# A graph network's second pass: another order of the turn on three engines, and step values loaded once per loop turn

## The chip, the cores and the metric

The kernel runs on 1 core of one Trainium2 chip. The metric is the device time of one execution in microseconds, as the median of 3 runs. Engines are called PE (TensorE), DVE (VectorE), ACT (ScalarE), POOL (GpSimd) and SP (SyncE).

## The reference

Four graph layers follow one another over 6,250 nodes and 206,250 edges sorted by `dst`. Each ends in a residual and a layer norm over 128 channels.

```python
x = _layernorm(x + _L0_gnn_ref(x, edge_index, edge_attr_128, ...))     # attention per edge, sum by dst
x = _layernorm(x + _L1_gnn_ref(x, edge_index_t, ...))                  # second layer: sums by src
x = _layernorm(x + _L2_gnn_ref(x, edge_index, edge_attr_128, ...))     # sum of edge features by src, small MLP
x = _layernorm(x + _L3_gnn_ref(x, ...))                                # top 8 of the edges of each src
```

The second layer needs, for each edge, the transformed row of one end and a sum over the edges that share the other end:

```python
h = jnp.matmul(node_states, kernel)
scores = jnp.exp(jnp.clip(leaky_relu(score_dst[dst] + score_src[src]), -2.0, 2.0))
out = jax.ops.segment_sum(h[src] * attention_norm[:, None], dst, num_segments=n_nodes)
```

(In this layer `dst` is `edges[:, 0]`, the kernel's `src`.) So the kernel must bring the edges from one order into the other. The part that does it, `stage_move`, is the one called the second pass here.

## The kernel before

Edges lie in tiles of 128, and 4 tiles are a group: there are 403 groups (GE). Nodes lie in 49 blocks of 128. Sorted edges touch their blocks in order, so a pass over pairs of group and block has 403 + 48 = 451 steps (KE). A table in SBUF, `steps`, holds for each step its group (row 0), its block (row 1) and its slot (row 2); an engine that needs one of these numbers for an address reads it into a register.

All loops are written with `pipeline(eng, n, *parts, ring=R)`. A part is `(function, lag)` or `(function, lag, items)`. In turn t an engine calls, in the order in which the parts are listed, each function for item t - lag. The middle of a loop runs as a hardware loop whose body is R turns; `u` is the item's place in the ring. Each engine works its own list in order and waits on semaphores that the others raise.

`stage_move` has two strands in one turn. The first ranks edges by their other end: one-hot tiles on DVE (`onehots`), their transposes and counts on PE (`counts`), the copy of the transposes on ACT (`turned`), running counts split into three bf16 parts (`running` on DVE, `high` on ACT, `below_high` on DVE, `middle` on ACT, `below_middle` on DVE), products on PE (`same`, `lookups`), and the choice of the place (`earlier`, `choose`, `position` on DVE, `index` on ACT). The second expands a node's row to its edges: ACT issues a DMA that broadcasts 512 keys to 128 partitions (`spread`, into 4 buffers `m_keys`), DVE compares them (`hot`), PE multiplies (`expand`), DVE adds the product into a slot of `m_rows` (`fill`), ACT adds three numbers (`put`). SP loads edge features into one of 8 slots (`load`, which raises `s_free`) and tells POOL when a group is complete (`ready`). POOL scatters it to DRAM by 4 indirect DMAs of 128 rows. The waits that the argument uses:

```python
spread: act.wait_ge(s_hot, k - U + 1)      # U = 4: the key buffer is free
turned: act.wait_ge(s_cnt, g + 1)          # PE counts(g) is done
expand: pe.wait_ge(s_add, k - 1); pe.wait_ge(s_hot, k + 1)   # fill(k - 2), hot(k)
hot:    dve.wait_ge(s_key[u], use * 16 + 16)
fill:   dve.wait_ge(s_got, k + 1); dve.wait_ge(s_free, g + 1)
below_middle: dve.wait_ge(s_middle, g + 1)
```

Two other loops read step values: `stage_aggregate` (first layer, 451 steps: SP loads, POOL weighs, DVE makes one-hots in `prepare` and adds in `add`, ACT copies, PE sums), and the last loop of `stage_last_layer`. There DVE keeps the block number of `prepare` for `add` where both fall into one loop body (class `Blocks`), and reads it again where not.

## Time and profile before

| | us |
|---|---|
| median of 3 runs | 14784.25 (14783.6 to 14784.43) |
| the profiled execution's own time | 14750.02 |
| its span in the profile | 14748.2 |

The span is the time from the first to the last instruction of one profiled execution. The execution's own time is 1.8 us longer than its span, and 34.2 us shorter than the median of the runs.

### The profile page before, as it was taken

What the parts mean: (1) busy time and instruction counts of PE and PEld (TensorE: products, weight loads), DVE (VectorE), ACT (ScalarE), POOL (GpSimd) and SP (SyncE); (2) the same over time, 40 slices, a digit from 0 to 9 for tenths busy, and PEclk for the clock granted to TensorE, in tenths of its full rate; (3) what the DMA queues carried; (4) which work ended last, traced back from release to release, by engine and by line L of the source; (5) the groups of instructions that cost most, each with busy time, mean ns of one, the idle gap of its engine ahead of it and who ended that gap; (6) DMA issues with size and microseconds to landing.
All of it is one profiled execution on the core that took longest, in us unless ns stands there. A gap on an engine that the chain in (4) does not pass through costs nothing. (4 is left out here: it accounts for less than half of the span.)

```text
span 14748.2 us, 216662 instructions
## 1 busy us (share of the span) xinstructions
PE 7244.2 (49%) x43137; PEld 6163.1 (42%) x43138; DVE 7073.5 (48%) x13194; ACT 1344.8 (9%) x4579; POOL 6702.6 (45%) x7772
## 2 busy tenths in 40 slices
PE   6999995673222222222222222223599578207543
PEld 4787774562222222222222222223366367206433
DVE  6444445776222222222222222222488678997535
ACT  1111111111000000000000000000011100001000
POOL 3777771663222222222222222225588057897773
PEclk9999998996555555555555555555799689657655
DMA  4777773451111111111111111114998069318654
GB/s 131 204 207 205 205 204 87 137 153 58 60 59 62 59 62 61 60 62 59 61 59 61 59 62 59 60 59 153 163 257 257 10 179 259 102 38 225 189 157 124
DMA packets 2114489, 1742.91 MB, mean 118 GB/s; under 512 B 377267, under 2 KB 1838644, under 8 KB 2114212
## 3 DMA queue, kind: packets, MB, share of 16 engines
q1 hardware_dynamic: 1220182, 819.70, 19.1%
q10 hardware_dynamic: 708032, 472.39, 12.2%
q0 software_dynamic: 186160, 449.72, 11.1%
q14 instruction: 96, 0.79, 0.0%
q8 instruction: 19, 0.31, 0.0%
HBM read 1289.54 MB, written 453.29 MB: 118 GB/s over the span
## 5 line engine op out<-in xcount | busy, mean ns | idle before, releaser
L1125 POOL DMA_INDIRECT sorted<-m_rows,srci x1612 | 1569.9, 974 | 5166.8 <-SPq L1112 4731.6
L1181 PE MATMUL m_psx<-held,m_hot 128*128 x3608 | 939.7, 441 | 4740.7 <-DVE m_rows L1335 4740.7
L1181 PEld LDWEIGHTS m_psx<-held,m_hot 128*128 128x128 f32 x3608 | 807.9, 329 | 4816.2 <-issue 4816.1
L1324 DVE TENSOR_SCALAR m_hot<-m_keys,node 128x512 f32<-128x512 int32 x451 | 225.7, 500 | 4583.0 <-DMA m_keys<-dst_row 4569.8
L1577 POOL DMA_INDIRECT z_xg<-table,srci x1664 | 2082.5, 1252 | 507.2 <-issue 507.2
L443 POOL DMA_INDIRECT g_xg<-table,srci x1612 | 1607.0, 997 | 491.1 <-issue 461.6
L1637 PE MATMUL z_ps<-z_wrow,z_oh 128*128 128x132 f32 x3712 | 757.8, 372 | 619.1 <-DVE z_wrow L1790 313.9
L462 PE MATMUL g_psg<-g_wg,g_eT 128*128 128x136 f32 x3224 | 1027.5, 474 | 0.0
L1452 PE MATMUL n_ps<-n_row,n_oh 128*128 128x257 f32 x3712 | 899.0, 391 | 249.4 <-DVE n_row L1428 203.4
L1637 PEld LDWEIGHTS z_ps<-z_wrow,z_oh 128*128 128x128 f32 x3712 | 666.7, 269 | 710.2 <-issue 670.2
L479 PE MATMUL g_psx<-scores,g_hot 128*128 x3608 | 840.2, 362 | 92.4 <-DVE e_score L568 87.0
L1452 PEld LDWEIGHTS n_ps<-n_row,n_oh 128*128 128x128 f32 x3712 | 670.9, 190 | 477.4 <-issue 347.6
L479 PEld LDWEIGHTS g_psx<-scores,g_hot 128*128 128x128 f32 x3608 | 806.7, 329 | 117.9 <-issue 115.1
L462 PEld LDWEIGHTS g_psg<-g_wg,g_eT 128*128 128x128 f32 x3224 | 769.3, 324 | 191.0 <-issue 191.0
L798 POOL TENSOR_TENSOR ag_wrow<-ag_buf,e_score 128x512 f32<-128x512 f32 x451 | 543.2, 1209 | 581.2 <-DMA ag_buf<-gated 359.4
L1206 ACT ACTIVATE m_ohtb<-m_pst 128x512 bf16<-128x512 bf16 x403 | 240.6, 597 | 5634.9 <-PE m_psu L1144 5634.9
L873 PE MATMUL ag_ps<-ag_wrow,ag_oh 128*128 128x136 f32 x3608 | 547.4, 299 | 233.2 <-DVE ag_oh L833 223.3
L1609 PE MATMUL z_ps<-z_tab,z_ohlo 128*128 128x200 bf16 x4992 | 601.3, 250 | 77.1 <-DVE z_e L1729 71.1
L541 DVE TENSOR_TENSOR g_y<-g_gate,g_xg 128x512 f32<-128x512 f32 x403 | 280.2, 695 | 732.5 <-DMA g_xg<-table,srci 731.5
L873 PEld LDWEIGHTS ag_ps<-ag_wrow,ag_oh 128*128 128x128 f32 x3608 | 466.0, 197 | 314.6 <-issue 197.0
L1171 PE MATMUL m_psl<-m_part,m_ohtb 128*128 128x100 bf16 x4836 | 582.8, 285 | 0.0
L833 DVE SCALAR_TENSOR_TENSOR ag_oh<-iota,blk,keys 128x512 f32<-128x512 f32 x451 | 470.6, 1044 | 181.6 <-PE ag_ps L873 97.3
(404 smaller groups left out, 13807.4 us busy)
## 6 DMA issues: line engine op xcount, KB each, us to landing
n_row<-sorted SPq DMA_DIRECT2D x464, 520.0 KB
z_buf<-gathered ACTq DMA_DIRECT2D x464, 256.0 KB, 3.6
g_keys<-dst_row ACTq DMA_DIRECT2D x451, 256.0 KB
ag_buf<-gated SPq DMA_DIRECT2D x451, 256.0 KB, 2.8
m_keys<-dst_row ACTq DMA_DIRECT2D x451, 256.0 KB, 3.7
gathered<-z_xg SPq DMA_DIRECT2D x416, 256.0 KB
gated<-g_y SPq DMA_DIRECT2D x403, 256.0 KB
g_eT<-in_attr_t SPq DMA_DIRECT2D x402, 256.0 KB
```

The lines of the kernel that those rows point to most:

```text
L443: nc.gpsimd.indirect_dma_start(out=xg[:, u, j, :], out_offset=None, in_=v.table[:, :], in_offset=bass.IndirectOffsetOnAxis(ap=v.srci[:, t: ...
L462: last = nc.tensor.matmul(psg[u % 2][:, h, j * W:(j + 1) * W], eT[:, u, (h * H + j) * P:(h * H + j + 1) * P], wg[:, :], start=False, stop= ...
L479: last = nc.tensor.matmul(psx[u % 2][:, j * X8:(j + 1) * X8], hot_t[:, u, j * P:(j + 1) * P], flat(v.scores[:, ds(b, 1), :]), start=True, ...
L798: engine.tensor_tensor(wrow[:, u, :, 0:C].rearrange("p t (h c) -> p t h c", h=heads), buf[:, u, :, :].rearrange("p t (h c) -> p t h c", h= ...
L873: last = nc.tensor.matmul(ps[u % 4][:, 0:width], oh[:, u, j, :], wrow[:, u, j, 0:width], start=(j == 0), stop=(j == G - 1))
L1125: nc.gpsimd.indirect_dma_start(out=v.sorted[:, :], out_offset=bass.IndirectOffsetOnAxis(ap=place[:, t:t + 1], axis=0), in_=rows[:, u, j, : ...
L1171: nc.tensor.matmul(to, ohtb[:, u, j * P:(j + 1) * P], before, start=(n == 0), stop=False)
L1181: last = nc.tensor.matmul(psx[u % 2][:, j // 2, (j % 2) * WH:(j % 2 + 1) * WH], hot_t[:, u, j * P:(j + 1) * P], flat(held[:, ds(b, 1), :]) ...
L1452: last = nc.tensor.matmul(ps[u % 4][:, 0:ROW], oh[:, u, j, :], row[:, u, j, 0:ROW], start=(j == 0), stop=(j == G - 1))
L1577: nc.gpsimd.indirect_dma_start(out=xg[:, u, j, :], out_offset=None, in_=v.table[:, :], in_offset=bass.IndirectOffsetOnAxis(ap=v.dsti[:, t: ...
L1609: nc.tensor.matmul(to, ohlo[:, u, edges], tab[:, n, :, :], start=(n == 0), stop=False)
L1637: last = nc.tensor.matmul(bank[u % 4 // 2][:, u % 2, 0:width], oh[:, u, j, :], wrow[:, u, j, 0:width], start=(j == 0), stop=(j == G - 1))
```

## The change

**Orders in `stage_move`.** On ACT `turned` goes from lag 0 to 2, `high` from 1 to 2, `middle` from 2 to 3, `index` from 5 to 6, `put` from 6 to 7; `spread` stays at 0 and first. On PE `expand` moves from the head of the turn to its end. On DVE `fill` moves from the end of the turn to second place. **Step values.** Class `StepRow` replaces single reads on the engines named below: at `u == 0` one instruction reads the values for all R turns of the loop body and for the `back` items before them. Code outside the hardware loop still reads one value at a time. PE's `expand` and SP's `ready` in `stage_move`, `stage_gate` and `stage_neighbours` keep their single reads.

```diff
-class Blocks:
...
+class StepRow:
+    def __init__(self, nc, eng, steps, row, top, back, ring, waited=False):
+        self.nc, self.eng, self.steps, self.row, self.top = nc, eng, steps, row, top
+        self.back, self.ring = back, ring
+        self.sure = None if waited else "stage_steps keeps groups and blocks in their ranges"
+
+    def turn(self, k, u):
+        if isinstance(k, int) or u:
+            return
+        _, self.values = self.nc.values_load_multi_w_load_instructions(
+            self.steps[0:1, self.row, ds(k - self.back, self.ring + self.back)], engines=[self.eng.engine], min_val=0,
+            max_val=self.top, skip_runtime_bounds_check_because=self.sure)
+
+    def at(self, k, u, lag=0):
+        if isinstance(k, int):
+            return self.eng.value_load(self.steps[0:1, self.row, ds(k, 1)], min_val=0, max_val=self.top)
+        return self.values[(u + lag) % self.ring - lag + self.back]
...
@@ stage_aggregate (the same form on SP, POOL, DVE, ACT; and on ACT and DVE in stage_last_layer)
-                blocks = Blocks(nc, dve, steps, groups, 3, R)
+                group = StepRow(nc, dve, steps, 0, groups - 1, 0, R)
+                node = StepRow(nc, dve, steps, 1, NBX - 1, 3, R)
...
@@ stage_move
-                pipeline(pe, GE, (expand, 1, KE), (lookups, 3), (same, 1), (counts, 0), ring=R)
+                pipeline(pe, GE, (lookups, 3), (same, 1), (counts, 0), (expand, 1, KE), ring=R)
...
+                ahead = StepRow(nc, act, steps, 0, GE - 1, 7, R, waited=True)
+                slots = StepRow(nc, act, steps, 2, S - 1, 7, R)
+
                 def spread(k, u, use):
-                    g, _ = step_of(nc, act, steps, k, GE)
+                    ahead.turn(k, u)
+                    slots.turn(k, u)
+                    g = ahead.at(k, u)
...
                 def put(k, u, use):
-                    g = act.value_load(steps[0:1, 0, ds(k, 1)], min_val=0, max_val=GE - 1)
-                    slot = act.value_load(steps[0:1, 2, ds(k, 1)], min_val=0, max_val=S - 1)
+                    g, slot = ahead.at(k, u, 7), slots.at(k, u, 7)
...
-                pipeline(act, GE, (spread, 0, KE), (turned, 0), (high, 1), (middle, 2), (index, 5), (put, 6, KE), ring=R)
+                pipeline(act, GE, (spread, 0, KE), (turned, 2), (high, 2), (middle, 3), (index, 6), (put, 7, KE), ring=R)
...
+                node = StepRow(nc, dve, steps, 1, NBX - 1, 0, R)
+                group, slots = StepRow(nc, dve, steps, 0, GE - 1, 3, R, waited=True), StepRow(nc, dve, steps, 2, S - 1, 3, R)
...
-                pipeline(dve, GE, (hot, 0, KE), (below_middle, 3), (choose, 4), (onehots, 0), (running, 1),
-                         (below_high, 2), (earlier, 2), (position, 4), (fill, 3, KE), ring=R)
+                pipeline(dve, GE, (hot, 0, KE), (fill, 3, KE), (below_middle, 3), (choose, 4), (onehots, 0), (running, 1),
+                         (below_high, 2), (earlier, 2), (position, 4), ring=R)
```

In ACT's loop body of `stage_move`, before, these instructions stand between the slot number's read (L1224), `put` (L1229), the next turn's `spread` (L343 reads, L1198 issues) and its `turned` (L1206). TENSOR_LOAD reads `steps` into a register, ISA and REGISTER_ALU work on registers.

```order
L1224 TENSOR_LOAD steps_e
L1224 ISA x2
L1225 REGISTER_ALU
L1229 ISA x2
L1229 ACTIVATE m_rows<-m_facts 128x4x3
L343 ISA
L343 TENSOR_LOAD steps_e
L343 ISA x2
L1198 ISA
L1198 DMA m_keys<-dst_row 128x512
L1205 REGISTER_ALU
L1206 ACTIVATE m_ohtb<-m_pst 128x512
```

After the change the head of ACT's loop body reads two rows of `steps` at once (11 values each: 7 back, 4 of the ring; L361), then comes `spread` (L1215) and the copies. The other three turns of the body have no TENSOR_LOAD.

```order
L361 TENSOR_LOAD steps_e
L361 ISA x23
L361 TENSOR_LOAD steps_e
L1212 REGISTER_ALU
L1215 ISA
L1215 DMA m_keys<-dst_row 128x512
L1220 REGISTER_ALU
L1222 REGISTER_ALU
L1223 ACTIVATE m_ohtb<-m_pst 128x512
L1226 REGISTER_ALU
```

Three single reads per turn became two reads per four turns, with 23 register instructions between them; the key DMA now stands directly behind the reads and ahead of a copy that belongs to a group two turns older.

On DVE, the end of a turn of `stage_move` before: `earlier` (L1303), `position` (L1316), two reads, `fill` (L1335).

```order
L1316 TENSOR_REDUCE m_facts<-m_mul 128x4x2
L1328 ISA
L1328 TENSOR_LOAD steps_e
L1328 ISA x2
L1329 ISA
L1329 TENSOR_LOAD steps_e
L1329 ISA x2
L1331 REGISTER_ALU
L1335 ISA
L1335 SCALAR_TENSOR_TENSOR m_rows<-m_rows,follows,m_psx 128x4x129
```

After the change, the seam between two turns: `position` (L1332), then `hot` (L1345) and `fill` (L1355) of the next turn, `below_middle` (L1312) and `choose` (L1326).

```order
L1332 TENSOR_REDUCE m_facts<-m_mul 128x4x2
L1345 ISA
L1345 TENSOR_SCALAR m_hot<-m_keys,node 128x512
L1351 REGISTER_ALU
L1355 ISA
L1355 SCALAR_TENSOR_TENSOR m_rows<-m_rows,follows,m_psx 128x4x129
L1312 TENSOR_TENSOR m_part<-m_rest,m_part 128x4x50
L1326 TENSOR_TENSOR m_mul<-m_psl,m_ohhi 128x400
```

`fill` moved from behind `position` to behind `hot`, and the reads between them are gone in three of four turns.

## Rows read from the trace of the kernel before

**Rows 1.** The page: span, busy time, granted clock and DMA by slice.
```profile
span 14748.2 us, 216662 instructions
PE 7244.2 (49%) x43137; PEld 6163.1 (42%) x43138; DVE 7073.5 (48%) x13194; ACT 1344.8 (9%) x4579; POOL 6702.6 (45%) x7772
...
PEclk9999998996555555555555555555799689657655
DMA  4777773451111111111111111114998069318654
...
L1206 ACT ACTIVATE m_ohtb<-m_pst 128x512 bf16<-128x512 bf16 x403 | 240.6, 597 | 5634.9 <-PE m_psu L1144 5634.9
```

**Rows 2.** Chain of waits, 4000 to 9000 us: us in total, times, longest.
```profile
ACT m_ohtb L1206 <- PE m_psu L1144: 4343.1, 310, 15.3
POOL sorted L1125 <- SPq L1112: 3615.7, 275, 28.4
PE m_psx L1181 <- DVE m_rows L1335: 3608.1, 311, 12.8
DVE m_hot L1324 <- DMA m_keys<-dst_row: 3533.9, 311, 12.6
ACT m_rows L1229 <- issue: 207.4, 310, 0.8
```

**Rows 3.** Timeline of one turn: start us, us, engine, line; idle before.
```profile
6001.67 0.60 ACT L1206 ACTIVATE m_ohtb<-m_pst 128x512 bf16<-128x512 bf16 x1 [13.24 <-PE m_psu L1144]
...
6003.56 0.21 ACT L1229 ACTIVATE m_rows<-m_facts  x1 [0.69 <-issue]
...
6004.36 0.34 ACTq L1198 DMA_DIRECT2D m_keys<-dst_row  x1
...
6008.05 0.48 DVE L1324 TENSOR_SCALAR m_hot<-m_keys,node 128x512 f32<-128x512 int32 x1 [10.82 <-DMA m_keys<-dst_row]
...
6010.69 0.35 DVE L1291 TENSOR_TENSOR m_rest<-m_cnt,m_part 128x200 f32<-128x200 f32 x1
...
6012.04 0.74 DVE L1335 SCALAR_TENSOR_TENSOR m_rows<-m_rows,follows,m_psx 128x516 f32 x1
...
6012.92 2.08 PE L1181 MATMUL m_psx<-held,m_hot 128*128 x8 [11.29 <-DVE m_rows L1335]
...
6017.65 0.60 ACT L1206 ACTIVATE m_ohtb<-m_pst 128x512 bf16<-128x512 bf16 x1 [13.87 <-PE m_psu L1144]
...
6018.40 0.36 ACT L1216 ACTIVATE m_part<-m_rest 128x200 bf16<-128x200 f32 x1
6018.66 0.20 ACT L1220 ACTIVATE srci<-m_facts  x1
```

**Rows 4.** Windows, 4000 to 9000 us.
```profile
4000.00:9000.00 5000.00, 1398.14 (x11187) 1327.45 (x11188) 1403.05 (x3110) 440.52 (x1550) 1082.47 (x1110) 0.57 0.18 60
```

**Rows 5.** Single reads on ACT, min/median/max ns: put's group, spread's.
```profile
L1223 ACTq FUSED_REGOPS  x588: 47/152/163, 3707.6 to 10302.3; - x196
L1223 ACTq TENSOR_LOAD <-steps_e x451: 275/281/742, 3707.3 to 10301.8; - x151
L1223 ACTq SEQ_ASSERT  x451: 18/18/18, 3707.8 to 10302.5; - x151
...
L343 ACTq TENSOR_LOAD <-steps_e x1353: 272/281/1484, 179.8 to 10275.8; - x194
```

**Rows 6.** Tile m_keys: from the DMA's issue to its landing.
```profile
DMA to landing us min/median/max: 3.0/3.7/5.5
```

**Rows 7.** Timeline at the stage's start, in its last turns and behind it.
```profile
3623.72 85.72 SPq L1106 DMA_DIRECT2D m_rows<-in_attr  x6
...
10292.73 0.96 POOL L1125 DMA_INDIRECT sorted<-m_rows,srci  x1 [0.30 <-SPq L1112]
...
10296.61 0.75 DVE L1335 SCALAR_TENSOR_TENSOR m_rows<-m_rows,follows,m_psx 128x516 f32 x1 [4.33 <-SPq L1101]
...
10297.79 0.96 POOL L1125 DMA_INDIRECT sorted<-m_rows,srci  x1 [0.30 <-SPq L1112]
...
10353.24 1.28 ACT L1400 ACT_TABLE_LOAD   x1 [46.22 <-PEq L1959]
```

**Rows 8.** POOL's indirect gathers in other stages: 1000 to 2000 us; last layer, page.
```profile
L443 POOL DMA_INDIRECT g_xg<-table,srci x772 | 765.8, 992 | 235.3 <-issue 219.4 <-DVE g_es L543 15.5 <-DVE g_y L541 0.3
...
L1577 POOL DMA_INDIRECT z_xg<-table,srci x1664 | 2082.5, 1252 | 507.2 <-issue 507.2
```

**Rows 9.** DVE's `prepare` in `stage_aggregate`: two steps' timeline rows, 8 steps apart.
```profile
2716.98 0.75 DVE L833 SCALAR_TENSOR_TENSOR ag_oh<-iota,blk,keys 128x512 f32<-128x512 f32 x1 [0.86 <-PE ag_ps L873]
...
2719.62 1.33 DVE L833 SCALAR_TENSOR_TENSOR ag_oh<-iota,blk,keys 128x512 f32<-128x512 f32 x1 [0.22 <-issue]
...
2721.08 1.33 DVE L833 SCALAR_TENSOR_TENSOR ag_oh<-iota,blk,keys 128x512 f32<-128x512 f32 x1
...
2730.75 0.75 DVE L833 SCALAR_TENSOR_TENSOR ag_oh<-iota,blk,keys 128x512 f32<-128x512 f32 x1 [0.86 <-PE ag_ps L873]
```

More of the change, by code:

```diff
@@ L806, in _ @@
             def _(sp):
+                group = StepRow(nc, sp, steps, 0, groups - 1, 0, R)
                 def loads(k, u, use):
-                    g, _ = step_of(nc, sp, steps, k, groups)
+                    group.turn(k, u)
+                    g = group.at(k, u)
                     load(sp, k, u, g)
@@ L814, in _ @@
             def _(pool):
+                group = StepRow(nc, pool, steps, 0, groups - 1, 0, R)
                 def weighted(k, u, use):
-                    g, _ = step_of(nc, pool, steps, k, groups)
+                    group.turn(k, u)
+                    g = group.at(k, u)
                     if later(k, R):
@@ L825, in _ @@
                 nc.vector.memset(acc[:, :, 0:width], 0.0).then_inc(s_z, 1)
-                blocks = Blocks(nc, dve, steps, groups, 3, R)
+                group = StepRow(nc, dve, steps, 0, groups - 1, 0, R)
+                node = StepRow(nc, dve, steps, 1, NBX - 1, 3, R)
                 def prepare(k, u, use):
-                    g, b = blocks.load(k, u)
+                    group.turn(k, u)
+                    node.turn(k, u)
+                    g, b = group.at(k, u), node.at(k, u)
                     if later(k, R):
@@ L838, in add @@
                 def add(k, u, use):
[L839 removed]
+                    b = node.at(k, u, 3)
                     dve.wait_ge(s_mm, k + 1)
@@ L852, in _ @@
                 nc.scalar.preload_act_table(ACT.Copy)
+                group = StepRow(nc, act, steps, 0, groups - 1, 0, R)
                 def put(k, u, use):
-                    g, _ = step_of(nc, act, steps, k, groups)
+                    group.turn(k, u)
+                    g = group.at(k, u)
                     if later(k, R):
@@ L1317, in position @@
                                             ALU.add).then_inc(s_pos, 1)
+                node = StepRow(nc, dve, steps, 1, NBX - 1, 0, R)
+                group, slots = StepRow(nc, dve, steps, 0, GE - 1, 3, R, waited=True), StepRow(nc, dve, steps, 2, S - 1, 3, R)
                 def hot(k, u, use):
-                    b = dve.value_load(steps[0:1, 1, ds(k, 1)], min_val=0, max_val=NBX - 1)
+                    for row in (node, group, slots):
+                        row.turn(k, u)
+                    b = node.at(k, u)
                     if later(k, U):
@@ L1327, in fill @@
                 def fill(k, u, use):
-                    g = dve.value_load(steps[0:1, 0, ds(k, 1)], min_val=0, max_val=GE - 1)
-                    slot = dve.value_load(steps[0:1, 2, ds(k, 1)], min_val=0, max_val=S - 1)
+                    g, slot = group.at(k, u, 3), slots.at(k, u, 3)
                     dve.wait_ge(s_got, k + 1)
@@ L1674, in stored @@
                     act.wait_ge(s_st[u % U], use * (16 * R // U) + 16 * (u // U + 1))
+                group = StepRow(nc, act, steps, 0, GS - 1, 0, R)
                 def load(k, u, use):
-                    g, _ = step_of(nc, act, steps, k, GS)
+                    group.turn(k, u)
+                    g = group.at(k, u)
                     if later(k, R):
@@ L1778, in _ @@
                 dve.wait_ge(s_z, 1)
-                blocks = Blocks(nc, dve, steps, GS, 3, R)
+                group = StepRow(nc, dve, steps, 0, GS - 1, 0, R)
+                block_row = StepRow(nc, dve, steps, 1, NBX - 1, 3, R)
                 def prepare(k, u, use):
-                    g, b = blocks.load(k, u)
+                    group.turn(k, u)
+                    block_row.turn(k, u)
+                    g, b = group.at(k, u), block_row.at(k, u)
                     if later(k, R):
```

16 lines of the change are left out of this document (1 added, 15 removed).

## The prediction

> **What bounds the kernel now.** I read the page's slices first: from about a quarter to two thirds of the span PE, DVE, ACT and POOL are all under three tenths busy and DMA stands at one tenth [rows 1]. That is `stage_move`. Nothing is full there, so the next view is the chain of waits in its middle: in 5000 us each engine waits 311 times for another, ACT for PE, PE for DVE, DVE for the keys' DMA, 11 to 14 us each time [rows 2]. The 311 turns take 5000 / 311 = 16.08 us each. The timeline of one turn shows a closed ring [rows 3]: ACT starts `turned` at 6001.67, has done all its copies and `put`, and issues the next keys at 6004.36 (2.69); they land and `hot` starts at 6008.05 (3.69); DVE works without a gap worth naming through nine instructions to `fill`, and PE starts `expand` at 6012.92 (4.87); PE ends `counts` and ACT's next `turned` starts at 6017.65 (4.73). Sum 15.98: every engine works in turn and no two at once. The reader is to see that the turn is long because of who stands behind whom. The key DMA of turn t + 1 needs nothing that `turned` of turn t makes; it stands behind it on ACT. `expand` needs `fill` of two steps back, which DVE does last in its turn, and `counts` stands behind `expand`.
>
> The stage lasts from 3623.7 to 10353.2, 6729.5 us [rows 7]. `turned` runs 403 times [rows 1]; 403 x 16.08 = 6480, which leaves 249.5 for the start, the last 48 steps and the drain. In these last steps DVE waits for a slot and POOL's groups follow at 10297.79 - 10292.73 = 5.06 us [rows 7]: POOL paces the end, before and after alike.
>
> **The ring after the change.** ACT issues `spread`(t) before `turned`(t - 2), DVE does `fill` right after `hot`, PE does `expand` last. Two loops are left.
>
> First, DVE's own work. From `hot` at 6008.05 to the end of `fill` at 6012.78 it is 4.73 us [rows 3]; I take 4.75 a turn. PE's turn was 4.7 us at a mean granted clock of 0.57 [rows 4], mostly the lower level (1.2 GHz). With one read (0.55, worked out below) it is 5.25 and fits if the turn is 5.3; `counts` no longer waits behind `expand`.
>
> Second, the keys. `spread`(t) stands behind `put` of ACT's turn t - 1; that turn holds `middle`(t - 4), which waits for `below_high`(t - 4), in DVE's turn t - 2. So one lap covers two turns: DVE from `hot` through `below_high` (6008.05 to 6011.04 = 2.99, plus `fill` 0.74 now ahead = 3.73), 0.1 to cross over (0.14 lie between `fill`'s end and `expand`), `middle` to the end of `put` (0.26 + 0.20 + 0.21 = 0.67), 0.15 to issue (now 0.59, of which the read goes), 3.9 to land (3.69 in this turn, median 3.7, maximum 5.5 [rows 6]; I add a little since the DMA share rises from 0.18 [rows 4] to 0.18 x 16.08 / 5.3 = 0.55). That is 8.55 for two turns, 4.28 each: less than DVE's 4.75. But once in four turns ACT reads its step values in this lap. Over four turns: two turns of DVE (9.5) and one lap, 18.05 + L, where L is the lump of reads.
>
> **What L costs.** A single read is 0.28 of load, 0.15 of register work and 0.02 of check, some 0.55 with the gaps [rows 5]. Before, ACT made three per turn, two between `index` and `put` (0.69 idle [rows 3]) and one ahead of `spread`. Now it makes two loads of 11 values, and one of them checks each value: 11 x (0.152 + 0.018) = 1.87. No row shows a load of many values. Lower bound: a load costs 0.28 whatever it brings, L = 0.56 + 1.87 = 2.4. Upper bound: 0.28 for each value, 22 x 0.28 + 1.87 = 8.0. A reason for less than nothing: ACT's sequencer may read ahead while `middle` waits, then L is hidden. I take 0.04 for each further value, near the lower end, since the values lie side by side in one row and the nearest row is one load with its whole round trip: L = 0.56 + 0.8 + 1.87 = 3.2. Then four turns are 21.25, one is 5.3 us; by the bounds 5.1 and 6.5.
>
> The Trainium skill (Runtime: NRT & Kernel Launch, Instruction fetch mechanics) speaks against the change here: it says that loading registers costs about 200 ns per register even in bulk. By that L would be 22 x 0.2 + 1.87 = 6.3, the turn 6.1, an estimate from that page, and the result about 10,690. The trace has no row to decide it. Its other page (DMA: Bandwidth & Descriptors, Latency and other measured facts) puts a floor of about 600 ns on such a load; the single loads here take half of that [rows 5], so the trace disagrees.
>
> DVE's lump (three loads of 4, 7 and 7 values, 7 checks, before `hot`) runs while the late keys are awaited, so it adds nothing to the lap. If L is hidden this cover is gone, and it costs up to 0.6 a turn.
>
> **What else moves.** `put` comes one turn later on ACT, so SP's `ready` and POOL's scatter do too. SP's list puts `load`(g + 8) behind `ready`(g + 3); `fill` of that group stands on DVE one turn after that `put`, where it was two. `put` ends 0.77 after `below_high`; DVE has `earlier`, `position` and `hot` (1.5) to do first, so it is covered. If it were not, up to 0.77 x 403 = 310 us. POOL needs 5.06 per group when alone and (765.8 + 235.3) / 772 x 4 = 5.19 beside busy engines [rows 8]; a turn brings 403 / 451 of a group, so POOL allows 4.64 per turn and does not pace.
>
> **Sum.** Stage: 403 x 5.3 + 249.5 = 2385, against 6729.5: -4344. `stage_aggregate`: 8 steps take 13.77 (2716.98 to 2730.75); where DVE has one read per step the pitch is 1.46 with no idle, where it has two it stands idle 0.86 [rows 9]. Without reads 8 x 1.46 = 11.7 plus a lump of 1 = 12.7: -1.07 per 8 steps, -60 over 451 (bounds: the lump hidden too -117, an expensive lump 0). POOL and DVE delay each other there (0.75 alone, 1.33 beside POOL), so nothing more. Last layer: POOL's gathers run nearly to its end (1664 of them, 2590 us [rows 8]) and pace it; only the last 50 steps or so gain: -10. Elsewhere nothing moves. Total -4414. From the profiled execution's own 14750.0 that is 10,336; the median of the runs is 34 above it: **10,370 us**.
>
> **Rivals.**
> 1. *Loads cost by the value.* L between 4.8 and 8.0, turn 5.7 to 6.5: 10,530 to 10,860. For: no row excludes it. Against: a single load is short. 0.20. This is the case that the page on launch in the Trainium skill describes.
> 2. *The landing slows.* With three times the traffic keys may take the maximum seen, 5.5: two-turn laps of 10.15, four turns 20.3 + 3.2 = 23.5, turn 5.9: 10,610. Or POOL runs as in the last layer, (2082.5 + 507.2) / 1664 x 4 = 6.23 per group; 403 groups are 2511, with 40 at the start 2550: 10,530. For: a DMA share of 0.55. Against: the maximum is rare, and beside a busy DVE in the first layer POOL kept 5.19. 0.15.
> 3. *The reads hide.* ACT reads ahead, turn 4.75 to 5.0, bound by DVE: 10,150 to 10,250. 0.12.
> 4. *The other side: slower.* The lump alone would have to eat the gain: 4 x 16.08 - 18.05 = 46 us, that is 2.0 us for each of 22 values. The longest single load seen is 1.48 [rows 5], the median 0.28. At 2.1 us a value the result is about 14,900. 0.02.
> 5. *The change does not do what it says*: the keys come early but some older wait closes the same ring, turn 16.08, 14,780. Four key buffers allow it (`spread`(t) needs only `hot`(t - 4)), and `turned` two turns later still finds its buffer of four. 0.01.
>
> **How the numbers follow.** The forecast (turn 5.0 to 5.7, 10,250 to 10,530) has 0.50. Its neighbours on both sides are near, so the range takes in rivals 2 and 3 and rival 1 up to 6.5 together with full price of everything else: 10,120 to 10,900. 0.2% of the time is 30 us, about what a measurement can tell from no change: faster 0.97, same 0.01, slower 0.02.
>
> **What would show it.** The stage should last about 2400 us with `hot` 5.3 us apart, DVE over eight tenths busy, POOL some seven tenths, and DMA share near 0.55. Right in detail, if in one turn of four `hot` waits for the keys, and in the others starts right after `position`. TENSOR_LOADs on ACT below 1 us each speak for L = 3.2, near 3 us for rival 1. Landings of keys above 5 us speak for rival 2. A granted clock near 1 would shorten PE's turn and change nothing; if it stays at 0.57, PE will be nearly as full as DVE. The prediction is wrong if ACT's `turned` or `high` turns out to wait for a younger instruction of DVE than the two-turn lap has it.

## Result and the profile after

| | us |
|---|---|
| kernel before, median of 4 runs | 14784.34 |
| changed kernel, median of 4 runs | 10870.01 (10841.36 to 10891.25) |
| ratio, 95% interval | 0.735 (0.733 to 0.737) |
| predicted | 10,370 (10,120 to 10,900) |

Faster by 3914 us. The result lies inside the range, 500 us above the forecast, and just above the stretch of 10,530 to 10,860 that rival 1 (*Loads cost by the value*) gave. A repeat (e9 below) gave 10,873 and 0.7359.

In three of the four sets of experiments below (the first, third and fourth) the kernel before took 17,156 to 17,175 us, not 14,780, and stages full of DMA moved 160 GB/s where they move 206 otherwise, so times and ratios are compared only between sets in which it took the same: one and the same kernel (e4) has a ratio of 0.790 in the first set and of 0.724 in the second.

The page of the changed kernel, which answers to [rows 1] (span, busy time, granted clock and DMA by slice):

```profile
span 10883.7 us, 199970 instructions
PE 6962.7 (64%) x43137; PEld 5914.6 (54%) x43138; DVE 7050.1 (65%) x13194; ACT 1374.6 (13%) x4579; POOL 6680.6 (61%) x7772
...
PEclk9999999996776777776777658999579965686556
DMA  3777777741552355455555589887049921487554
```

The long valley is gone. `stage_move` now goes from SP's first load to the table load that follows it (source lines L1118 and L1420; min/median/max ns, first and last start):

```profile
L1118 SPq DMA_DIRECT2D m_rows<-in_attr x402: 367/373/452, 3623.1 to 6410.3; - x134
L1420 ACT ACT_TABLE_LOAD  x1: 1283/1283/1283, 6462.1 to 6462.1; - x1
```

6462.1 - 3623.1 = 2839.0 us against 6729.5 [rows 7]: 3890.5 less, nearly the whole difference of the spans (3864.5). It starts at the same time as before, so `stage_aggregate` and what stands ahead of it gave nothing; behind it the rest takes 4421.6 instead of 4395.0, 27 more. The turn is (2839.0 - 249.5) / 403 = 6.42 us, not 5.3.

The timeline shows where the 1.1 is. This is `hot` over four turns and two bodies' first key DMAs, with ACT's copies around them (start us, us, engine, line; idle before):

```profile
5001.02 0.34 ACTq L1215 DMA_DIRECT2D m_keys<-dst_row  x1
5001.60 0.60 ACT L1223 ACTIVATE m_ohtb<-m_pst 128x512 bf16<-128x512 bf16 x1 [8.98 <-issue]
...
5004.45 0.49 DVE L1345 TENSOR_SCALAR m_hot<-m_keys,node 128x512 f32<-128x512 int32 x1 [6.84 <-DMA m_keys<-dst_row]
...
5008.64 0.21 ACT L1245 ACTIVATE m_rows<-m_facts  x1
5008.81 0.34 ACTq L1215 DMA_DIRECT2D m_keys<-dst_row  x1
5009.10 0.48 DVE L1345 TENSOR_SCALAR m_hot<-m_keys,node 128x512 f32<-128x512 int32 x1
...
5013.74 0.48 DVE L1345 TENSOR_SCALAR m_hot<-m_keys,node 128x512 f32<-128x512 int32 x1
...
5017.91 0.21 ACT L1245 ACTIVATE m_rows<-m_facts  x1
...
5018.37 0.48 DVE L1345 TENSOR_SCALAR m_hot<-m_keys,node 128x512 f32<-128x512 int32 x1
...
5026.83 0.34 ACTq L1215 DMA_DIRECT2D m_keys<-dst_row  x1
5027.41 0.60 ACT L1223 ACTIVATE m_ohtb<-m_pst 128x512 bf16<-128x512 bf16 x1 [9.29 <-issue]
```

Three turns are 4.65, 4.64 and 4.63 apart: DVE works through without a wait, as forecast (4.75). In a turn without reads the key DMA goes out where `put` starts its last 0.2 (5008.64 and 5008.81). In the fourth it goes out 8.71 us after `put` is done (5018.12 to 5026.83): that is the lump. From one body's first key DMA to the next are 25.81 us; less 18.05 for two turns of DVE and one lap, L is 7.8, where the sum had 3.2. (Read directly, the lump is the 8.7; the rest of the four turns took 17.1 where the sum had 18.05 less 0.15 for the issue, so 7.8 is what the sum's own terms leave for it.) The loads themselves (source line L361, ACT and DVE; min/median/max ns):

```profile
L361 ACTq FUSED_REGOPS  x1335: 51/147/158, 3690.2 to 10668.0; - x191
L361 ACTq SEQ_ASSERT  x1177: 18/18/18, 3690.4 to 6358.9; - x197
...
L361 DVEq TENSOR_LOAD <-steps_e x432: 347/1624/2541, 2670.0 to 6376.0; - x144
L361 ACTq TENSOR_LOAD <-steps_e x269: 544/2800/3433, 2636.6 to 6359.0; - x135
```

ACT has two kinds of loads there: 8 values in `stage_aggregate` (0.54) and 11 in `stage_move` (2.80). Two of 2.80 and the checks' 1.87 are 7.47; the rest is gaps and register work. Eleven values thus cost 0.25 each, and eight 0.07 each, and that is the question for the experiments. For the other forecasts, here are the chain of waits from 4000 to 5000 us, to be set beside [rows 2], the window from 4000 to 6000 us, beside [rows 4], and the landing of the keys, beside [rows 6]:

```profile
ACT m_ohtb L1223 <- issue: 355.3, 39, 9.5
POOL sorted L1137 <- SPq L1124: 295.7, 77, 10.5
DVE m_hot L1345 <- DMA m_keys<-dst_row: 269.0, 40, 7.5
ACT m_part L1229 <- DVE m_cnt L1300: 254.6, 113, 3.6
```
```profile
4000.00:6000.00 2000.00, 1183.21 (x11232) 1066.78 (x11232) 1388.78 (x3120) 465.28 (x1560) 1100.29 (x1113) 0.73 0.52 151
```
```profile
DMA to landing us min/median/max: 3.0/3.4/7.6
```

`hot` waits for keys 40 times in 1000 us, once in four turns (1000 / 25.8 = 38.8). DVE is 0.69 busy, not over 0.8, and POOL 0.55, not seven tenths; the DMA share is 0.52 (0.55 forecast). The granted clock is 0.73, between its two levels (1.2 and 2.4 GHz), where the stretch was at 0.57 before.

`stage_aggregate`, DVE's `prepare` as in [rows 9]:

```profile
2809.32 1.65 DVE L842 SCALAR_TENSOR_TENSOR ag_oh<-iota,blk,keys 128x512 f32<-128x512 f32 x1 [2.65 <-issue]
...
2818.78 1.33 DVE L842 SCALAR_TENSOR_TENSOR ag_oh<-iota,blk,keys 128x512 f32<-128x512 f32 x1
...
2822.97 1.65 DVE L842 SCALAR_TENSOR_TENSOR ag_oh<-iota,blk,keys 128x512 f32<-128x512 f32 x1 [2.65 <-issue]
```

Eight steps take 13.65 (13.77 before). The idle time of single reads is replaced by one of 2.65, in which DVE reads 8 and 11 values.

### The profile page after: what moved, and what is told of

Read it like the earlier page. It is cut to its first block and busy times, and to the rows that moved or that the text cites. A ratio compares the mean times of both kernels' runs of the same rounds, so it can differ in the third digit from the quotient of the medians.

```text
span 10883.7 us, 199970 instructions
## 1 busy us (share of the span) xinstructions
PE 6962.7 (64%) x43137; PEld 5914.6 (54%) x43138; DVE 7050.1 (65%) x13194; ACT 1374.6 (13%) x4579; POOL 6680.6 (61%) x7772
## 5 line engine op out<-in xcount | busy, mean ns | idle before, releaser
L1657 PE MATMUL z_ps<-z_wrow,z_oh 128*128 128x132 f32 x3712 | 733.4, 368 | 654.6 <-DVE acc L1828 285.4
L1193 PE MATMUL m_psx<-held,m_hot 128*128 x3608 | 750.4, 373 | 183.3 <-DVE m_rows L1355 112.9
L1193 PEld LDWEIGHTS m_psx<-held,m_hot 128*128 128x128 f32 x3608 | 645.5, 269 | 226.2 <-issue 217.9
L1168 PE MATMUL m_psq<-m_ohtb 128*128 128x128 bf16 x1612 | 200.8, 264 | 884.8 <-ACT m_ohtb L1223 611.3
L1345 DVE TENSOR_SCALAR m_hot<-m_keys,node 128x512 f32<-128x512 int32 x451 | 222.4, 493 | 759.9 <-DMA m_keys<-dst_row 705.1
L885 PE MATMUL ag_ps<-ag_wrow,ag_oh 128*128 128x136 f32 x3608 | 585.9, 338 | 197.8 <-DVE ag_oh L842 188.2
L885 PEld LDWEIGHTS ag_ps<-ag_wrow,ag_oh 128*128 128x128 f32 x3608 | 572.6, 245 | 211.1 <-issue 191.5
L842 DVE SCALAR_TENSOR_TENSOR ag_oh<-iota,blk,keys 128x512 f32<-128x512 f32 x451 | 534.1, 1185 | 157.4 <-issue 150.7
L1816 DVE TENSOR_TENSOR z_wrow<-z_buf,z_e 128x512 f32<-128x512 f32 x464 | 319.2, 688 | 486.1 <-DMA z_buf<-gathered 486.1
```

The costliest lines, as they stand in the source:

```text
L842: nc.vector.scalar_tensor_tensor(oh[:, u, :, :], v.iota[:, None, :].broadcast_to([P, G, P]), v.blk[:, ds(b, 1)], keys[:, ds(g * G, G), Non ...
L885: last = nc.tensor.matmul(ps[u % 4][:, 0:width], oh[:, u, j, :], wrow[:, u, j, 0:width], start=(j == 0), stop=(j == G - 1))
L1193: last = nc.tensor.matmul(psx[u % 2][:, j // 2, (j % 2) * WH:(j % 2 + 1) * WH], hot_t[:, u, j * P:(j + 1) * P], flat(held[:, ds(b, 1), :]) ...
L1657: last = nc.tensor.matmul(bank[u % 4 // 2][:, u % 2, 0:width], oh[:, u, j, :], wrow[:, u, j, 0:width], start=(j == 0), stop=(j == G - 1))
```

## Experiments

The theories named in the expectations: **A**, a read costs by the number of its values; **B**, what counts is where in the row it starts (a multiple of four is cheap); **C**, what counts is whether the number is a multiple of four. A rival to all: the lump doesn't matter, DVE or POOL sets the 6.42.

### First set: parts of the change by themselves

**e1_sizes.** The changed kernel with a small stage of reads of many sizes, whose values nothing uses.

```diff
+                row(16, 1)
+                row(16, 2)
...
+                row(16, 16)
```

> The changed kernel with one small stage added behind the first layer's table of steps: SP, ACT and DVE each read 1, 2, 4, 7, 8, 11, 12 and 16 values of the table at once, from starts 16, 17, 18 and 20, three times over, each form on a line of its own. Theory A, a load costs by the value: about 0.28 us and 0.25 us for each further value whatever the start, so 8 values 2.0 us, 11 values 2.8 us, 16 values 4.0 us. But the changed kernel's trace shows 8 values read in 0.55 us in the aggregate loop and 11 values in 2.8 us. Theory B, the start decides: reads whose start is a multiple of 4 or 8 values are short at any length (8 values 0.55 us, 12 values about 0.7 us), reads from starts 17 and 18 cost 0.25 us a value (8 values 2.0 us). Theory C, the number decides: 4, 8 and 16 values are short from any start (under 0.9 us), 7, 11 and 12 values cost 0.25 us each (1.7, 2.8, 3.0 us) from any start.

Measured: 13,832 us in one run. Loads whose values nothing used left no instruction in the program, so it says nothing on sizes. It serves as the changed kernel in this set: 0.805 of the kernel before, `stage_move` 7726.8 - 4244.1 = 3483 us.

**e4_orders_only.** All new orders, single reads in `stage_move`.

```diff
-                    ahead.turn(k, u)
-                    slots.turn(k, u)
-                    g = ahead.at(k, u)
+                    g, _ = step_of(nc, act, steps, k, GE)
...
-                    g, slot = ahead.at(k, u, 7), slots.at(k, u, 7)
+                    g = act.value_load(steps[0:1, 0, ds(k, 1)], min_val=0, max_val=GE - 1)
+                    slot = act.value_load(steps[0:1, 2, ds(k, 1)], min_val=0, max_val=S - 1)
```

(DVE's `hot` and `fill` alike. The grouped reads of the other loops stay, here and in e5, e6 and e7.)

> The three new orders in stage_move with single reads as before (0.55 us each, three per turn on ACT and on DVE); the other loops keep their grouped reads. If the lump of two reads of 11 values with 11 checks (about 8 us once in four turns) is what made the turn 6.42 us where I forecast 5.3, the turn falls to DVE's own work of 4.65 to 5.3 us, the stage from 2839 to 2130 to 2390 us, and the whole to 10,160 to 10,420 us. If instead slower landings or crowding on POOL or DMA set the turn, it stays near 6.4 us and the whole near 10,870 us; if the grouped reads helped in stage_move, it is slower than the changed kernel.

Measured: 13,562 us (13,531 to 13,583), ratio 0.790 (0.789 to 0.792). Without grouped reads in this stage it is faster than the changed kernel. The expected times hold for the condition of the result and can't be compared here; the second set repeats the kernel in it (e4_again), and there the turn is 5.99, not 4.65 to 5.3.

**e5_act_order_only.** As e4, and PE and DVE keep their old orders.

```diff
-                pipeline(pe, GE, (lookups, 3), (same, 1), (counts, 0), (expand, 1, KE), ring=R)
+                pipeline(pe, GE, (expand, 1, KE), (lookups, 3), (same, 1), (counts, 0), ring=R)
```

> ACT's new order alone in stage_move, single reads there, PE's and DVE's orders as before. Worked out lap by lap with the trace's durations: the keys are early, but PE still begins its turn with expand, which waits for fill at the end of DVE's turn, and DVE's choose waits for lookups behind expand: turn 6.8 us, stage 3000 us, whole 11,030 us. If ACT's order is all that matters the time is that of the run with all three orders, 10,160 to 10,420 us; if PE and DVE matter as much as ACT, the turn is above 10 us and the whole above 12,400 us.

Measured: 14,361 us (14,326 to 14,371), ratio 0.836 (0.834 to 0.837). ACT's order alone brings most. What is left is told by its timeline:

```profile
6006.86 2.08 PE L1193 MATMUL m_psx<-held,m_hot 128*128 x8 [5.15 <-DVE m_rows L1353]
...
6016.29 2.08 PE L1193 MATMUL m_psx<-held,m_hot 128*128 x8 [4.87 <-DVE m_rows L1353]
```

A turn is 9.43 us (6006.86 to 16.29): PE begins with `expand`, which waits for `fill`, and `fill` is DVE's last. Keys are no longer in the ring, the two of PE and DVE are. I had expected a turn of 6.8 and a stage of 3000 us; the stage took 8261.6 - 4243.1 = 4018.5. How much of that miss is the ring and how much this set's condition, in which ACT also waits 80 times in 1000 us for a releaser that the trace doesn't name, isn't shown.

**e7_reads_only.** Old orders on all engines, grouped reads (ACT back 6).

```diff
-                ahead = StepRow(nc, act, steps, 0, GE - 1, 7, R, waited=True)
-                slots = StepRow(nc, act, steps, 2, S - 1, 7, R)
+                ahead = StepRow(nc, act, steps, 0, GE - 1, 6, R, waited=True)
+                slots = StepRow(nc, act, steps, 2, S - 1, 6, R)
...
-                pipeline(act, GE, (spread, 0, KE), (turned, 2), (high, 2), (middle, 3), (index, 6), (put, 7, KE), ring=R)
+                pipeline(act, GE, (spread, 0, KE), (turned, 0), (high, 1), (middle, 2), (index, 5), (put, 6, KE), ring=R)
```

> The old orders on all three engines with the grouped reads of the change (put at its old lag of 6, so 10 values per read on ACT). The ring of four engines stays closed, and the lump on ACT lies in it: three reads of 0.55 us per turn go, of which 1.2 us were exposed, and some 7.5 us come once in four turns, so 0.7 us more per turn: 16.7 us, whole 14,950 to 15,100 us. Rival: grouped reads are a gain by themselves, 16.08 minus 1.2 us a turn at best, 14,300 us.

Measured: 16,995 us (16,972 to 17,006), ratio 0.990 (0.988 to 0.992): not slower by 1 to 2%, as I had expected, but nearly the same. The closed ring stays, and its turns show both sides of the grouping:

```profile
6003.17 0.49 DVE L1345 TENSOR_SCALAR m_hot<-m_keys,node 128x512 f32<-128x512 int32 x1 [15.58 <-DMA m_keys<-dst_row]
...
6017.39 0.49 DVE L1345 TENSOR_SCALAR m_hot<-m_keys,node 128x512 f32<-128x512 int32 x1 [9.49 <-DMA m_keys<-dst_row]
```

The turn without reads is 14.22, some 2 us shorter than 16.08; in the turn with the reads `hot` waits 6 us longer (15.58 against 9.49). Three times some 2 less and once some 4 more (20.3) than 16.08: hardly anything is left. The mean turn of the stage is (10874.0 - 4205.8 - 249.5) / 403 = 15.93. The 16.08 comes from the trace of the other condition, so this comparison holds only as far as that does not change the closed ring.

### Second set: what a read costs

Here the kernel before took 14,775 us (14,763 to 14,782), as in the result.

**e9_changed_again.** The changed kernel with no edit, as control.

```diff
 (no edit)
```

> The changed kernel itself, so that the others of this call stand beside it on the same chip. In its own result it took 0.735 of the kernel before, with stage_move 2839 us. On the chip of the first call, where the kernel before took 17175, one run of it took 13832. Here, if the chip is like the first, 10,870; if it is like the second, some 13,830. Either way it should stand 2% above the next kernel but one (new orders with single reads), as it did there.

Measured: 10,873 us (10,857 to 10,886), ratio 0.7359 (0.7347 to 0.7371); `stage_move` 6463.1 - 3623.8 = 2839.3.

**e8_sizes.** The small stage again, now with each sum of values used as an address; one source line for each form.

```diff
+                for _ in range(2):
+                    use(load(steps[0:1, 0, 16:17], ...)[1])     # L357
+                    use(load(steps[0:1, 0, 16:18], ...)[1])     # L358
...
+                    use(load(steps[0:1, 0, 16:32], ...)[1])     # L373
```

> The changed kernel with one small stage more, in which ACT and DVE each read 1, 2, 4, 7, 8, 11, 12 and 16 values from starts at 16 (a multiple of four), 17, 18 and 20, every form twice. Theory A (by the value): durations rise with the number whatever the start, 11 values 2.8 and 16 values 4. Theory B (by the start): from 16 or 20 all forms take 0.3 to 1.0; from 17 the same numbers of values take 0.25 us for each. Theory C (by the number): 4, 8, 12 and 16 are cheap from any start; 7 and 11 dear from any start.

The whole took 10,942 us in one run. Measured, on ACT (source lines; min/median/max ns). In order: values 16:20, 17:21, 16:23, 16:24, 17:25, 17:28, 16:32:

```profile
L360 ACTq TENSOR_LOAD <-steps_e x2: 316/316/316, 167.3 to 192.6; - x2
...
L362 ACTq TENSOR_LOAD <-steps_e x2: 918/919/920, 169.5 to 194.7; - x2
...
L363 ACTq TENSOR_LOAD <-steps_e x2: 977/987/997, 170.9 to 196.1; - x2
...
L365 ACTq TENSOR_LOAD <-steps_e x2: 552/552/553, 174.4 to 199.6; - x2
...
L368 ACTq TENSOR_LOAD <-steps_e x2: 1764/1764/1764, 178.8 to 204.0; - x2
...
L370 ACTq TENSOR_LOAD <-steps_e x2: 2397/2400/2404, 182.9 to 208.1; - x2
...
L373 ACTq TENSOR_LOAD <-steps_e x2: 1019/1019/1019, 188.6 to 213.8; - x2
```

Beside these, 18:22 took 0.920 like 17:21, 20:28 took 0.554 like 16:24, 17:24 took 1.558, 16:27 took 1.218, 16:28 took 0.789, and two values 0.496 from 16 and from 17. Theory B is right, save that the number counts too. Four values take 0.316 from 16 and 0.92 from 17 or 18; eight 0.552 from 16 or 20 and 1.764 from 17; eleven 1.22 and 2.40. From a multiple of four each further group of four costs (1.019 - 0.316) / 3 = 0.234, that is 0.06 a value, and what is left over at the end (3 values in 16:23 and 16:27) 0.22 a value. From any other start every value costs it: (2.400 - 0.919) / 7 = 0.21. A fails on eight values from 16 and from 17 (0.552 against 1.764), and C on the same pair. The changed kernel reads 11 values from k - 7 with k a multiple of four in the body: the dearest form.

**e2_back_of_four.** One value more per read, so that the start is a multiple of four.

```diff
-                ahead = StepRow(nc, act, steps, 0, GE - 1, 7, R, waited=True)
-                slots = StepRow(nc, act, steps, 2, S - 1, 7, R)
+                ahead = StepRow(nc, act, steps, 0, GE - 1, 8, R, waited=True)
+                slots = StepRow(nc, act, steps, 2, S - 1, 8, R)
...
-                group, slots = StepRow(nc, dve, steps, 0, GE - 1, 3, R, waited=True), StepRow(nc, dve, steps, 2, S - 1, 3, R)
+                group, slots = StepRow(nc, dve, steps, 0, GE - 1, 4, R, waited=True), StepRow(nc, dve, steps, 2, S - 1, 4, R)
```

> In stage_move the reads bring more values, but start at a multiple of four in the row: ACT 12 instead of 11, DVE 8 instead of 7. Theory A (a read costs by its number of values, about 0.25 each beyond a small number): ACT's reads take 3.0 each instead of 2.8, the lump grows by some 0.4 + 0.17, four turns by 0.6, stage_move by 60 us. Theory B (the start decides: reads of 4 and of 8 values from a multiple of four or eight take 0.35 to 0.6 in the trace of the changed kernel, those of 7 and 11 from elsewhere 1.7 and 2.8): ACT's reads fall to 0.7 each or less, the lump to 0.7 x 2 + 1.87 = 3.3, four turns to 18.05 + 3.3 = 21.3, one turn to 5.3, stage_move by 1.1 x 403 = 440 us. Theory C (it is a matter of the number alone, multiples of four are cheap and others are split into single values): same as B here; the run of sizes tells B and C apart.

Measured: 10,514 us (10,509 to 10,550), ratio 0.7116 (0.7104 to 0.7128): 359 us less than the changed kernel in the same set. `stage_move` takes 6137.6 - 3630.3 = 2507.3, a turn 5.60. Its reads (L361), and the first and last `hot` of four turns with the key DMA between:

```profile
L361 ACTq TENSOR_LOAD <-steps_e x269: 539/787/1142, 2643.8 to 6031.4; - x135
```
```profile
5013.12 0.48 DVE L1345 TENSOR_SCALAR m_hot<-m_keys,node 128x512 f32<-128x512 int32 x1 [4.06 <-DMA m_keys<-dst_row]
...
5027.07 0.50 DVE L1345 TENSOR_SCALAR m_hot<-m_keys,node 128x512 f32<-128x512 int32 x1
...
5031.59 0.34 ACTq L1215 DMA_DIRECT2D m_keys<-dst_row  x1
...
5035.28 0.49 DVE L1345 TENSOR_SCALAR m_hot<-m_keys,node 128x512 f32<-128x512 int32 x1 [3.48 <-DMA m_keys<-dst_row]
```

A read of 12 takes 0.79 where one of 11 took 2.80. Four turns are 22.16, so L is 22.16 - 18.05 = 4.1 against 7.8: 3.7 less, where two reads shorter by 2.01 and one check more give 4.02 - 0.17 = 3.85. B's expectation (the stage shorter by 440) was 108 too high: it left out some 0.5 us of gaps in the lump and took the turn of the changed kernel a little too long. Read directly, 4.8 us stand between the end of `put` and the key DMA (5026.81 to 5031.59) where the changed kernel had 8.7. The edit changes the starts of the reads on ACT and on DVE and nothing else, and in both kernels DVE's reads are done before the late `hot`: by 2.2 us in the changed kernel (its last read ends at 5002.2), by 0.3 here (5035.0). This shows that ACT's lump, not DVE's work or POOL, makes the step from 5.6 to 6.4. Here DVE's own reads have become nearly as late as the keys.

**e4_again.** e4_orders_only, beside the changed kernel.

```diff
-                    g, slot = group.at(k, u, 3), slots.at(k, u, 3)
+                    g = dve.value_load(steps[0:1, 0, ds(k, 1)], min_val=0, max_val=GE - 1)
+                    slot = dve.value_load(steps[0:1, 2, ds(k, 1)], min_val=0, max_val=S - 1)
```

> New orders, but single reads as before in stage_move. In the first call it took 13,562 where the changed kernel took 13,832 in one run. If the grouped reads cost more than they save, it is faster again than the changed kernel of this call by 250 to 650 us (stage_move by 403 turns x 0.65 to 1.6); if the first call's difference was one of runs, the two are within 30 us.

Measured: 10,687 us (10,673 to 10,723), ratio 0.7243 (0.7228 to 0.7258): 186 us faster than the changed kernel, less than expected, 174 slower than e2. `stage_move` is 6250.4 - 3587.7 = 2662.7, a turn 5.99. DVE's timeline:

```profile
5004.92 0.50 DVE L1342 TENSOR_SCALAR m_hot<-m_keys,node 128x512 f32<-128x512 int32 x1
5006.78 0.75 DVE L1353 SCALAR_TENSOR_TENSOR m_rows<-m_rows,follows,m_psx 128x516 f32 x1 [1.35 <-SPq L1113]
...
5011.12 0.69 DVE L1342 TENSOR_SCALAR m_hot<-m_keys,node 128x512 f32<-128x512 int32 x1
```

From `hot` to `hot` are 6.20 here, and the turn's largest gap is the one ahead of `fill`, where DVE's two single reads stand. The waits from 4000 to 5000 us say the same:

```profile
DVE m_rows L1353 <- SPq L1113: 95.9, 84, 1.5
...
DVE m_rows L1353 <- issue: 55.8, 67, 1.6
...
DVE m_hot L1342 <- DMA m_keys<-dst_row: 19.1, 38, 1.2
```

151 gaps of 1.0 us in 1000 us, nearly one for each of the 167 turns, while `hot` waits for keys only 19.1 us in all: DVE bounds this kernel by its own work of 4.64 and by its reads, which make up 5.6 of the 5.99. (About half of the gaps have SP as their releaser. But in the turn shown the two reads ahead of `fill`, source lines L1346 and L1347, and their register work run from 5004.9 to 5006.4 and so fill the gap; and in e6 below the same gap is 1.34 and named issue.)

### Third and fourth set: PE and DVE alone, and another place for the reads

**e6_pe_dve_orders_only.** Single reads, ACT's old order, new orders on PE and DVE.

```diff
-                pipeline(act, GE, (spread, 0, KE), (turned, 2), (high, 2), (middle, 3), (index, 6), (put, 7, KE), ring=R)
+                pipeline(act, GE, (spread, 0, KE), (turned, 0), (high, 1), (middle, 2), (index, 5), (put, 6, KE), ring=R)
```

> Single reads, ACT's old order, the new orders on PE and DVE alone. The keys' DMA still stands behind put and ahead of turned. Of the ring of four engines only the place of fill and expand changes: hot -> counts -> turned stays, with the keys' landing in it. Worked out lap by lap with the durations of the trace of before: turn 12.05, stage_move 5100, the whole some 13,150. The rival: one engine's order does nothing without the other's, turn 16, 14,700. With the first call's ACT order alone (0.836 of before) it tells which part of the change carries how much.

Measured: 16,278 us (16,261 to 16,286), ratio 0.948 (0.947 to 0.950). One turn:

```profile
6000.99 0.49 DVE L1342 TENSOR_SCALAR m_hot<-m_keys,node 128x512 f32<-128x512 int32 x1 [7.49 <-DMA m_keys<-dst_row]
6002.82 0.75 DVE L1353 SCALAR_TENSOR_TENSOR m_rows<-m_rows,follows,m_psx 128x516 f32 x1 [1.34 <-issue]
...
6008.29 0.60 ACT L1221 ACTIVATE m_ohtb<-m_pst 128x512 bf16<-128x512 bf16 x1 [11.62 <-PE m_psu L1156]
6011.13 0.34 ACTq L1213 DMA_DIRECT2D m_keys<-dst_row  x1
...
6014.78 0.49 DVE L1342 TENSOR_SCALAR m_hot<-m_keys,node 128x512 f32<-128x512 int32 x1 [7.62 <-DMA m_keys<-dst_row]
```

The turn is 13.79, not 12.05. The ring of ACT, keys, DVE and PE's `counts` stays closed; PE's `expand` left it, but `fill` and its two reads (0.75 and 1.34) now stand in it, ahead of `onehots`. I had left that out; together they are 2.1 us, which covers the miss of 1.7. The mean turn of the stage is 14.1. ACT's order alone is 0.836, PE's and DVE's 0.948, both together 0.790; 1 - 0.164 - 0.052 = 0.784, so in this condition the parts nearly add.

**e11_spread_first.** From e2: ACT reads 4 values ahead of `spread` and 8 + 8 behind it; register bounds in place of checks.

```diff
-                    ahead.turn(k, u)
-                    slots.turn(k, u)
+                    ahead.turn(k, u)                       # 4 values, from k
...
                         [P, G * P])).then_inc(s_key[u], 16)
+                    group.turn(k, u)                       # 8 values, from k - 8
+                    slots.turn(k, u)
```

> The kernel with starts at a multiple of four, and in stage_move three things more: ahead of the key DMA of the body's first turn ACT reads only the 4 group numbers of the ring (0.32), unchecked; the 8 group and 8 slot numbers of past steps that put needs (0.55 each) are read behind that DMA; in place of a check for each value (0.17) the four numbers that a wait uses are bounded by one register instruction each. DVE reads one row of 4 ahead of hot and two of 8 behind it. If the lump ahead of the key DMA is what is left of the reads' cost (one lap of two turns in four carries 3.8 us in the kernel before this one), ACT's lap loses 3.4 us in four turns and DVE's own work becomes the bound: 4 x 4.75 plus its reads of 0.35 + 0.6 + 0.6 + some 0.6 = 21.2, a turn of 5.3 against 5.6: 120 us less than e2_back_of_four. If the reads' place doesn't matter (DVE or POOL already bounds), it is within 30 us of e2_back_of_four.

Measured: 13,569 us (13,540 to 13,586), ratio 0.790 (0.789 to 0.792). The expectation of 120 us less than e2 can't be judged, since e2 has no run in this condition.

**e12_spread_first_dve_ahead.** The same, DVE's reads ahead of `hot`.

```diff
+                    for row in (node, group, slots):
+                        row.turn(k, u)
```

> The same as e11_spread_first, but DVE's three reads all stay ahead of hot. If hot of the body's first turn still waits for keys, they hide there and this is faster than e11_spread_first by up to 1.7 us in four turns (170 us); if DVE never waits for keys any more, the two take the same within 30 us.

Measured: 13,539 us (13,535 to 13,549), ratio 0.789 (0.788 to 0.790). `stage_move` is 3255 us here and 3261 in e11: the place of DVE's reads makes no difference that can be seen here; most of the 30 us between the two lies in `stage_aggregate` (742 and 773 us, see the last section). Nor is either better than the orders with single reads, at 0.790 in the first set. Against e2's 0.7116 nothing can be said, since e2 ran in the other condition. There the waits (5000 to 6000 us of e12) are of another kind:

```profile
ACT m_ohtb L1250 <- remote: 464.1, 60, 9.0
POOL sorted L1162 <- SPq L1149: 384.6, 61, 11.1
DVE m_mul L1353 <- remote: 312.3, 56, 6.3
```

Between them turns run at the full pace of 4.64 (`hot` at 6003.17 and 6007.81), and about twice per loop body DVE and PE stand still together for 5 to 6 us, and ACT for 7 to 8, with a releaser that the trace doesn't name. These stops hide what was to be seen. What they are, no run here shows.

**e13_best.** e12, and DVE's block numbers in `stage_aggregate` and the last layer from a multiple of four (12 instead of 11).

```diff
-                node = StepRow(nc, dve, steps, 1, NBX - 1, 3, R)
+                node = StepRow(nc, dve, steps, 1, NBX - 1, 4, R)
```

> e12_spread_first_dve_ahead, and in stage_aggregate and the last layer DVE reads its 12 block numbers from k - 4 instead of 11 from k - 3. By the measured sizes each of these reads falls from 2.5 to 0.85. In stage_aggregate that is 1.7 us of 2.65 idle once in 8 steps: 56 of these are 95 us if DVE paces it, and nothing if POOL and DVE hold each other up there. In the last layer, where gathers and loads pace, 0 to 100. If this chip is like that of the result (before 14,780), stage_move should stand at 2360 to 2400 us: spread ahead of the long reads takes 3.4 us of 4 turns off the lap, DVE's reads hide while keys are awaited. Sum: 0.7116 of before (the kernel with starts at a multiple of four) less 120 and 95 us is 0.697 to 0.71. If DVE's own work and POOL already bound stage_move, it stays within 30 us of 10,514 plus what stage_aggregate gives. If the chip is like that of the call before, 0.789 less 0 to 0.010.

Measured: 13,428 us (13,421 to 13,431), ratio 0.7826 (0.7813 to 0.7839), 0.006 below e12, 110 us. The matmuls of `stage_aggregate` run from 3227.6 to 3952.6, 725 us against 742 in e12, and the last layer's DVE steps 753 us against 846; together these are the 110, as expected (95 and 0 to 100). Of all kernels measured here, e13 has the lowest time of the sets in which the kernel before took some 17,160 us, and e2_back_of_four in the other. Whether e13 is faster than e2 isn't shown.

## Why the prediction came out as it did

**Right: the bound and the ring.** The turn of before was a closed ring, and opening it made `stage_move` 3890 us shorter. ACT's order, which takes the key DMA out of the ring, is the larger part (0.836 alone, 0.948 for PE's and DVE's, 0.790 for all three). Three turns in four stand at 4.64 (4.75 forecast), in the fourth `hot` waits for keys; this is the detail that was named. The start, last steps and drain as the same 249.5 fit: 403 x 6.45 + 249.5 = 2849, measured 2839.

**Wrong in size: L.** The step was "I take 0.04 for each further value, near the lower end", which gave L = 3.2. By the sum's other terms L came out at 7.8 (2 x 2.80 + 1.87 = 7.47, and the rest gaps); read directly, the lump is 8.7. The term's error is 4.6 us in four turns, 1.15 a turn, 463 us over 403; in the stage 2839 - 2385 = 454. The whole miss is 454 there, 60 in `stage_aggregate` and 37 in the last layer (below), less 49, since this profiled execution lies 15 above the median where the one of before lay 34 below: 502 of the 500 measured. The upper bound in the text, 0.28 a value, L = 8.0, turn 6.5, is where it fell. I argued from the single load that a load is one round trip. The rows of before held nothing on many values, and what decides, the start of the load, did not stand in my sum at all. With the start at a multiple of four, twelve values cost 0.79 (e2), 0.05 for each further value, close to what I took; there L is 4.1 (loads 1.58, 12 checks 2.04, gaps 0.5) and the turn 5.60 by the stage, 5.54 by the timeline.

**The page and the trace.** The Trainium skill (Runtime: NRT & Kernel Launch, Instruction fetch mechanics) states about 200 ns per register even in bulk. The trace agrees for starts off a multiple of four (0.21, e8) and disagrees for starts on one (0.06). The page speaks of registers that the launch code loads from HBM; the loads here read a table in SBUF, so that the figures meet may be chance. By that page the forecast was 10,690; it was the nearer one.

**DVE's lump.** "Runs while the late keys are awaited, so it adds nothing": in the changed kernel, right; DVE stands 6.84 us idle there, and its last read ends at 5002.2, 2.2 us before `hot` starts. In e11 and e12 its place made no difference to be seen either.

**`stage_aggregate` (-60).** Not there: 8 steps 13.65 against 13.77. The row of idle 0.86 twice in eight steps went, but one of 2.65 came, the unforeseen price of 11 values from k - 3. The bound "an expensive lump 0" held. **Last layer (-10):** it became 27 longer, with one idle stretch of 3.48 in eight steps ahead of `prepare`. It isn't shown that this is the cause of all 27.

**Rivals.** 1 is what happened to these reads, which all start off a multiple of four, and, but for 10 us, its numbers held; I had given it 0.20 against 0.50. As a rule for every load it is wrong (e8). 2 (landing) did not come: median 3.4. The maximum rose from 5.5 to 7.6, and three turns in four stayed at 4.64 all the same. (In e2, with its shorter turns, the median is 4.3.) Its other half, a slower POOL, did not come either: four scatters are 3.95 us busy and have some 1.3 us of gaps, 5.2 a group (5.19 forecast, 6.23 in the rival). 3 (reads hide) was excluded by the 9 us ahead of `turned`. 4 and 5 did not come.

**What the grouping is worth.** It is not the part that made the kernel faster. On the new orders, grouped reads as the change has them cost 186 us against single ones (e9 and e4_again), and with a good start they save 174 (e2). In `stage_move` alone these are 177 and 155 us; `stage_aggregate` was 32 us shorter in e4_again than in the other two. Under the old order they are worth at most 1% (e7).

**Open.** Why the kernel before takes 2,380 us more in three sets, and what stops three engines together twice a body there. The trace of e7 shows only where the time goes while the ring is closed: 4206 us lie ahead of `stage_move` (3623 in the changed kernel of the result) and 6096 behind it (4422), while the turn itself is no longer than 16.08. Whether spread-first beats e2 where these stops are absent was not tried again.

## What to carry to other kernels

A ring of waits is opened by moving what needs nothing of the turn (a load of keys) ahead of what waits for that turn; look for who stands behind whom, engine by engine, and count what you move into the ring as well as what leaves it. Registers loaded in bulk want their start at a multiple of four: twelve values from one took 0.79 us where eleven from elsewhere took 2.40 (e8). A lump once per loop body costs most of its length if it stands ahead of a transfer that others wait for: of the 8.7 us, 25.81 - 4 x 4.64 = 7.3 came through. To put in front of the transfer only the values that it needs follows from this, but e11, which does it, has not shown a gain.

## What the runs showed of the hardware

- A load of n values from SBUF into ACT's registers: 0.32 for four from a multiple of four, 0.234 for each further four, and 0.21 to 0.22 for each value outside such a group; 16 values 1.02, 11 from an odd place 2.40 (e8). DVE: 0.35, 1.10 and 2.50. In the busy `stage_move` the 11 take 2.80. A single load is 0.28, two values cost more than four (0.496 against 0.316).
- `stage_aggregate` ran at one of two paces in programs whose code for this stage is the same: its matmuls took 774 us in the changed kernel (2639.9 to 3413.7), e9 and e2, and 742 in e4_again (2637.1 to 3379.1). A second run of each program kept its pace (774 in e1, 742 in e4_orders_only), and e11 and e12, which differ only in `stage_move`, had 773 and 742. The granted clock from 2750 to 3300 us was 0.75 in the first and 0.88 in the second, but in the kernel before, at 771 us (2643.7 to 3414.3), it was 0.98, so the clock alone does not tell it. What sets it isn't shown; differences of 30 us between these kernels can come from it.
